# An attention + fp4 feed-forward block on one core: loads moved between two stacks of DMAs, and one small copy issued by ScalarE's own queue

## The reference

```
for each of the 16 batches b:
    q = layernorm(x[b])                       # no gain, no bias; eps 1e-5
    k = v = ctx[b]
    x1[b] = x[b] + softmax(q k^T / 4) v       # 16 heads of 16 channels
for each row of x1:
    z = layernorm(x1)
    h = silu(fp4(z) fp4(w_gate)^T) * (fp4(z) fp4(w_up)^T)    # 704 wide
    out = x1 + fp4(h) fp4(w_down)^T
# fp4: blocks of 16 along the last axis, scale = max|block| / 6, values on
# the grid 0, .5, 1, 1.5, 2, 3, 4, 6
```

## Time and profile before

| | |
|---|---|
| median of 3 runs | 541.68 us (538.37 to 542.48) |
| profiled execution, its own time | 540.0 us |
| its span | 538.2 us |
| attention: from the first scores of step 1 to those of step 13 | 53.82 to 230.52 us |
| mean granted TensorE clock | 0.975 |

### The profile page before, as it was taken

The page is one execution under the profiler, slowest core; times in us unless marked ns, Lnnn a source line. Parts: engine busy times, 40 slices in busy tenths (PEclk is TensorE's granted clock), DMA queues, the critical chain, the costliest instruction groups (busy, mean ns, idle before and its releaser), DMA issues.

```text
span 538.2 us, 13724 instructions
## 1 busy us (share of the span) xinstructions
PE 492.4 (91%) x4036; PEld 382.7 (71%) x4036; DVE 442.3 (82%) x1129; ACT 371.2 (69%) x739; POOL 306.0 (57%) x424
## 2 busy tenths in 40 slices
PE   1885999999999999999776799999999999999996
PEld 0232556556566666655445699999999999999996
DVE  3786799899998999988444789888899888899764
ACT  5355798989998999977663465666656665656653
POOL 7636566646556565533415565667666667666543
PEclk9999799999999999999876999999999999999999
DMA  7749658666667666530000000000000000000000
GB/s 213 221 131 234 185 141 226 191 174 185 185 184 186 187 196 196 154 102 22 3 0 2 0 12 21 19 19 19 10 19 19 19 19 19 10 19 21 22 22 29
DMA packets 49985, 48.97 MB, mean 91 GB/s; under 512 B 4768, under 2 KB 47648, under 8 KB 49952
## 3 DMA queue, kind: packets, MB, share of 16 engines
q1 hardware_dynamic: 49952, 48.58, 31.9%
HBM read 18.94 MB, written 4.19 MB: 43 GB/s over the span
## 4 chain that ended last, share of the span: by engine, by line
PE 72%; DVE 7%; SPq 5%; issue 5%; DMA 4%; POOL 3%; ACT 3%; DVEq 0%; POOLq 0%; ACTq 0%
PE SC L1172 21%; PE PV L1172 12%; PE PV L1120 9%; PE MX L1102 9%; PE SC L1088 8%; DVE MF L776 4%; PE T L1197 4%; SPq L299 3%; DMA QS<-MT 2%; PE T L1202 2%; PE T L1069 2%; PE T L1037 1%; PE SC L1197 1%; DMA KT<-in_ctx_t 1%; PE T L1044 1%
## 5 line engine op out<-in xcount | busy, mean ns | idle before, releaser
L776 DVE TENSOR_REDUCE MF<-MX 128x2 f32<-128x512 f32 x256 | 165.8, 683 | 20.9 <-PE MX L1102 17.3
L609 ACT ACTIVATE P<-SC 128x512 f32<-128x512 f32 x256 | 140.8, 593 | 26.8 <-PE SC L1088 25.2
L1102 PE MATMUL MX<-KS,QS 96*128 96x256 bf16 x512 | 104.3, 288 | 7.1 <-DVE MF L776 5.3
L1088 PE MATMUL SC<-QS,KS 98*128 98x256 bf16 x512 | 100.9, 280 | 5.9 <-DMA QS<-MT 5.8
L532 POOL TENSOR_TENSOR HQ<-HN,hscale 128x704 f32<-128x704 f32 x31 | 43.1, 1391 | 60.5 <-DVE HN L928 60.5
L1120 PE MATMUL PV<-P,VA 128*32 128x256 f32 x1024 | 72.0, 401 | 0.5 <-ACT OT L618 0.5
L1088 PEld LDWEIGHTS SC<-QS,KS 98*128 98x128 bf16 x512 | 44.2, 99 | 39.0 <-ACT P L609 17.3
L709 ACT ACTIVATE HH<-T 128x768 fp32r<-128x768 f32 x31 | 25.2, 813 | 67.1 <-PE T L1197 67.1
L1102 PEld LDWEIGHTS MX<-KS,QS 96*128 96x128 bf16 x512 | 43.3, 100 | 38.2 <-DVE MF L776 29.1
L1172 PE MATMUL SC<-WH,XH 128*128 128x352 f32 x256 | 68.3, 348 | 0.0
L1172 PE MATMUL SC<-WH,XL 128*128 128x352 f32 x256 | 62.6, 326 | 0.0
(11 more groups left out here) (137 smaller groups left out, 1034.4 us busy)
## 6 DMA issues: line engine op xcount, KB each, us to landing
KS<-KP SPq DMA_DIRECT2D x96, 128.0 KB, 2.9
QS<-QP SPq DMA_DIRECT2D x96, 128.0 KB, 2.4
QN<-in_x_p SPq DMA_DIRECT2D x16, 256.0 KB, 3.0
KT<-in_ctx_t SPq DMA_DIRECT2D x16, 256.0 KB, 3.1
C<-in_ctx SPq DMA_DIRECT2D x16, 256.0 KB, 4.2
X<-in_x SPq DMA_DIRECT2D x16, 256.0 KB, 4.6
out<-OB SPq DMA_DIRECT2D x32, 128.0 KB, 1.7
W<-in_L_ffn_w_down SPq DMA_DIRECT2D x2, 352.0 KB, 3.4
```

The source lines that it names most:

```text
L609: nc.scalar.activation(P[g % 2][:, j, :, :], SC[h % 3][:, :, :], ACT.Exp, scale=0.25).then_inc(exp_done, 1)
L776: nc.vector.tensor_reduce(MF[st.slot(off, 2)][:, :, h:h + 1], MX[h % 2][:, :, :], AX.X, ALU.max, negate=True).then_inc(mx_done, 1)
L1088: last = nc.tensor.matmul(SC[h % 3][:, k, :], KS[r][0:ROWS, h, k * 128:(k + 1) * 128], QS[r][0:ROWS, h, :], start=True, stop=True)
L1102: last = nc.tensor.matmul(MX[h % 2][:, q, :], QS[r][0:PROD, h, q * 128:(q + 1) * 128], KS[r][0:PROD, h, :], start=True, stop=True)
```

## The change

- **SyncE's order in a step** becomes: K stack, loads, Q stack, weights. The load of x is that of batch t and not t+1. The load of queries and keys of batch 3 (`load_first(3, 3)`) moves ahead of the first step. In step -1 the first weights come before the Q stack.
- **MT** is no longer in SyncE's order: ScalarE waits for its own copy to MT and issues the DMA itself, right behind it.
- **The rows of ones**: GpSimd writes KS[0] and KS[1] in step -2, one after the other, and KS[2] in step -1 once `v_ready` and `m_parts` (the maxima's low part of batch 0 on VectorE) are there. ScalarE writes KS[3] in step -1 at slot (1, 2), with one ACTIVATE over 2x4096 elements of a broadcast source, scale 0 and bias 1.
- **VectorE** waits for w_down's load at slot (3, 3) of step 4, and no longer at (1, 1).

```diff
--- before.py
+++ after.py
@@ -214,7 +214,7 @@
         w_zeroed, w_begun, w_loaded = sem("w_zeroed"), sem("w_begun"), [sem(f"w_loaded{m}") for m in range(3)]
         w_seq, w_scaled, w_abs, w_c, w_grid, w_done = (sem(n) for n in
             ("w_seq", "w_scaled", "w_abs", "w_c", "w_grid", "w_done"))
-        ones_ready = sem("ones_ready")
+        ones_ready, ones_last = sem("ones_ready"), sem("ones_last")
         w_tr, w_out = sem("w_tr"), sem("w_out")
         zeroed = sem("zeroed")
         wh_out = sem("wh_out")
@@ -350,16 +350,9 @@
             load_context(0, 0)
             sp.wait_ge(w_zeroed, 4)
             load_blocks(0, wg_in, 0, 2, w_begun)
+            load_first(3, 3)
 
             def attention_step(st):
-                if st.first >= 0 and st.has(RING):
-                    sp.wait_ge(v_ready, st.times(0, 1, 1))
-                    gate(sp)
-                    load_first(st.item(RING), st.slot(RING, RING))
-                if st.first >= 0 and st.has(2):
-                    load_context(st.item(2), st.slot(2, RING))
-                if st.first >= 0 and st.has(1):
-                    load_x(st.item(1), st.slot(1, RING))
                 if st.has(LEAD):
                     r = st.slot(LEAD, RING)
                     sp.wait_ge(k_low, st.times(LEAD, 1, 1))
@@ -367,22 +360,22 @@
                     sp.wait_ge(sc_ready, st.times(0, H, 1))
                     gate(sp)
                     stack(KS[r], KP[st.slot(LEAD, 2)], (0, 1, 2, 0, 1, 0), r)
-                if st.has(1):
-                    sp.wait_ge(mt_ready, st.times(1, 1, 1))
+                if st.first >= 0 and st.has(RING):
+                    sp.wait_ge(v_ready, st.times(0, 1, 1))
                     gate(sp)
-                    r = st.slot(1, 2)
-                    sp.dma_start(QS[st.slot(1, RING)][PROD:ROWS, :, :].rearrange("d h t -> d (h t)"),
-                                 MT[r][:, :]).then_inc(m_stacked[r], 16)
+                    load_first(st.item(RING), st.slot(RING, RING))
+                if st.has(2):
+                    load_context(st.item(2), st.slot(2, RING))
+                if st.has(0):
+                    load_x(st.item(0), st.slot(0, RING))
                 if st.first == -1:
-                    load_first(3, 3)
+                    load_weights(-1)
                 if st.has(LEAD):
                     sp.wait_ge(q_out, st.times(LEAD, 3, 3))
                     gate(sp)
                     stack(QS[r_q(st)], QP[st.slot(LEAD, 2)], (0, 0, 0, 1, 1, 2), r_q(st))
-                if st.first == -1:
-                    load_context(1, 1)
-                    load_x(0, 0)
-                load_weights(st.first)
+                if st.first >= 0:
+                    load_weights(st.first)
 
             def r_q(st):
                 return st.slot(LEAD, RING)
@@ -428,13 +421,11 @@
                 nc.gpsimd.memset(WD[:, r, FI:], 0.0).then_inc(w_zeroed, 1)
             pool.wait_ge(w_zeroed, 4)
 
-            def row_of_ones(r, st):
-
-                pool.wait_ge(k_low, st.first + LEAD + 1)
-                if st.has(1):
-                    pool.wait_ge(v_ready, st.first + 2)
-                nc.gpsimd.memset(KS[r][PROD:ROWS, :, :], 1.0).then_inc(ones_ready, 1)
-                pool.wait_ge(ones_ready, r + 1)
+            def rows_of_ones(rs):
+
+                for r in rs:
+                    nc.gpsimd.memset(KS[r][PROD:ROWS, :, :], 1.0).then_inc(ones_ready, 1)
+                    pool.wait_ge(ones_ready, r + 1)
 
             def attention_step(st):
                 if st.has(-2):
@@ -474,8 +465,13 @@
                     nc.gpsimd.tensor_scalar(VA[r][:, :, :, 0:DK],
                                             C[rc][:, :, :].rearrange("p q (h d) -> p q h d", d=DK),
                                             1.0, 0.0, ALU.mult, ALU.add).then_inc(v_ready, 1)
-                if 1 - LEAD <= st.first < 1 - LEAD + RING:
-                    row_of_ones(st.first + LEAD - 1, st)
+                if st.first == 1 - LEAD:
+                    pool.wait_ge(k_low, 2)
+                    rows_of_ones((0, 1))
+                if st.first == -1:
+                    pool.wait_ge(v_ready, 1)
+                    pool.wait_ge(m_parts, 1)
+                    rows_of_ones((2,))
                 if st.has(GRID):
 
                     ws = wslice(st, GRID)
@@ -598,6 +594,10 @@
                 if st.first + 1 >= 2:
                     act.wait_ge(m_stacked[r], st.turn(-1, 2, 16))
                 nc.scalar.activation(MT[r][:, :], TA16[0:2 * H, 0:S], ACT.Copy).then_inc(mt_ready, 1)
+                act.wait_ge(mt_ready, st.times(1, 1, 1))
+                gate(act)
+                nc.scalar.dma_start(QS[st.slot(1, RING)][PROD:ROWS, :, :].rearrange("d h t -> d (h t)"),
+                                    MT[r][:, :]).then_inc(m_stacked[r], 16)
 
             def exp(st, g, j):
                 if not st.has(0):
@@ -655,6 +655,11 @@
                         if (g, j) == (1, 2) and st.has(LEAD):
                             for q in range(QT):
                                 normalise(st, q)
+                        if (g, j) == (1, 2) and st.first == -1:
+                            act.wait_ge(consts, IDENTS)
+                            nc.scalar.activation(KS[RING - 1][PROD:ROWS, :, :].rearrange("d h t -> d (h t)"),
+                                                 ident[PROD:ROWS, 0:1].to_broadcast([ROWS - PROD, H * S]),
+                                                 ACT.Identity, bias=1.0, scale=0.0).then_inc(ones_last, 1)
                         if (g, j) == (2, 0) and st.first < 0:
                             maxima_out(st)
                         for n, at in enumerate(((2, 0), (2, 3), (3, 3))):
@@ -835,7 +840,6 @@
                     dve.wait_ge(w_loaded[0], 32)
                 elif st.first == RING:
                     dve.wait_ge(w_loaded[1], 48)
-                    dve.wait_ge(w_loaded[2], 32)
                 dve.wait_ge(w_scaled, st.times(SCALE, 1))
                 nc.vector.tensor_reduce(wmax[:, :], blocks(wslice(st, SCALE)), AX.X, ALU.max,
                                         apply_absolute_value=True).then_inc(w_seq, 1)
@@ -896,6 +900,8 @@
                             output(st, 1)
                         if (g, j) == ((3, 2) if st.first > 0 else (3, 3)) and st.has(SCALE):
                             weight_inverses(st)
+                        if (g, j) == (3, 3) and st.first == RING:
+                            dve.wait_ge(w_loaded[2], 32)
                         if st.first == B - 1 and HG * g + j < LOTS:
                             weights_out(HG * g + j)
 
@@ -1080,8 +1086,10 @@
                     if st.first == 0:
                         pe.wait_ge(ones_ready, 1)
                         pe.wait_ge(consts, CONSTS)
-                    if st.first in (1, 2, 3):
+                    if st.first in (1, 2):
                         pe.wait_ge(ones_ready, st.first + 1)
+                    if st.first == RING - 1:
+                        pe.wait_ge(ones_last, 1)
 
                 pe.wait_ge(exp_done, st.times(0, H, h - 2 if h > 2 else (0, -2, -1)[h]))
                 for k in range(QT):
```

## The result

| | median, us | range | runs | ratio to before, 95% interval |
|---|---|---|---|---|
| before | 538.67 | 535.1 to 542.48 | 20 | |
| changed | 543.13 | 541.39 to 545.65 | 20 | 1.0093 (1.007 to 1.0115) |

The change makes the kernel 0.9% slower. The median of before is that of 20 runs here; the 541.68 us given further up was of three. The profiled execution of the changed kernel took 542.69 us, with a span of 540.8 (before 540.0 and 538.2), so the two traces differ by 2.6 us, and this is what follows accounts for.

What follows compares the result with a forecast made beforehand. TensorE, busy 91% of the span, was taken as the bound, with ScalarE short of slack. 540.0 - 13.6 won + 7.0 paid = 533.4 us, or 534.5 for the middle of the runs; range 529 to 541.

Steps and rivals of the forecast that it cites:

- Loads behind the K stack: Each step, SyncE's order: four loads fit between K stack and Q stack, KT lands in time; cost put at nothing.
- (a): Before step 1: MT issued earlier by ScalarE lands before TensorE ends step 0; all 4.46 us of idle time go.
- MT on ScalarE's queue: Steps 0 to 14: issue and lost overlaps delay ScalarE 0.94 us, 0.55 us of pitch in steps 1 to 12; 7.0 us together.
- The first sum: Ahead of step 1: idle time before it, VectorE's slow cast and a TensorE stall in step 0 go; 6.8 us won.
- (b): Step -1: VectorE's cast of the maxima, no longer held by GpSimd's memset, takes 0.17 us instead of 1.47; 1.30 us won.
- (c): Step 0: the memset of ones is gone, and with it TensorE's stall at 47.36; 1.03 us won.
- The second sum: Steps 1 to 12: time above twelve pitches of 14.16 us (slow clock, w_down wait, late MT, memset) goes; 6.8 us won.
- Rival 2: Each step: ScalarE's issue waits for SyncE's, pitch grows by 1.18 us; 541 us, with half 537, written as 539; chance 0.20.
- Rival 3: Each step: the Q stack lands late behind the loads, pitch 16.0 at a 5.77 us landing; 548 us, slower; chance 0.10.
- Rival 4: Step 1: MT comes no sooner, the backlog being in the 16 engines; idle time and half clock stay; 540.5 us; chance 0.07.

## Why the prediction was wrong, point by point

**What bounds the kernel** was read rightly: TensorE, with ScalarE next in line and short of slack, and it is there that the kernel lost.

**The step that failed: "Loads behind the K stack ... Nothing, with the rival below."** I followed the landing of KT, of x and of the Q stack, and not that of MT, which the same loads are issued beside. In step (a) I had taken 2.8 us from the earlier trace rows as its flight, a row where MT has the K stack's tail ahead and no load after it, and set it down as good for the new order. It is 3.87 us. Of the pitch of 15.34, 14.88 is there with MT on ScalarE alone, so 0.46 us a step, 5.5 us in all, come from this. It was put at nothing, and it is the largest single miss: with it the profiled execution would have been forecast at about 539 us, and not at 533.4. The same "nothing" covered KT, and there too it is wrong at a pitch of 14.16 us, where ScalarE waited for KT for up to 3.27 us; the changed kernel's long step hides that.

**MT on ScalarE's queue: mechanism right, size off.** The exponentials and the copy of PV were pushed back, values at (3, 3) waited for the latter, and it was paid in each step. Forecast 0.94 us of delay for 0.55 of pitch, measured 0.72. The issue itself took 0.64 (0.69 taken); behind it ScalarE needs 0.2 us more before it starts, for which I had 0.1, so with the lost overlap the delay is 1.05 us. The pitch was mis-sized by 0.72 - 0.55 = 0.17 us, and 0.17 x 12 = 2 us.

**The first sum, 6.8 us ahead of step 1, came out as 4.35.** (a) The idle 4.46 us are gone, but through the order and not the queue (5.44 us under way with the old order). (b) The cast took 0.18 us:

```profile
27.29 0.18 DVE L802 CAST MP<-MF 128x32 bf16<-128x32 f32 x1
```

and the transposes of the maxima came 1.5 us earlier. That was lost at once: ScalarE's first issue, 1.49 us, held up the queries' part behind it, TensorE's next weights waited for that part, and the first scores came at 33.66, before at 33.55. The products at 31.33, with 1.28 us of idle time before them, name VectorE as their releaser; the weight load ahead of them names ScalarE's part:

```profile
30.92 0.10 PEld L1050 LDWEIGHTS T<-QP,negidentb 128*128 128x128 bf16 x1 [1.35 <-ACT QP L570]
```

(c) The stall in step 0 went, and two waits for ScalarE (0.51 and 0.45) took its place. So of the 2.44 us missing from this sum 1.41 are lost ahead of the first scores of step 0 and 1.03 between these and step 1.

**The second sum, 6.8 us above the pitch,** is gone as forecast in the changed kernel, since the longer pitch hides all small irregularities. Where the pitch is short, with MT on SyncE, 172.73 us for twelve steps leave 2.8 us, with the landings of the Q stack and of KT among them.

**The rivals.** Rival 2 gave the right pitch, 15.34 (14.16 + 1.18), and the right time within 2 us (541 with its full price), but by a mechanism that didn't occur: the issue took 0.64 us with SyncE's own beside it, so no wait for the other sequencer shows, and the shared generator of the Trainium skill, Perfetto Trace Analysis, section "DMA Instruction - HWDGE (DVE, Sync)", isn't needed to explain anything here. Rival 3 had the right cause, landings lengthened by the loads, and the wrong transfer. In the changed kernel the Q stack lands 2.5 us after its issue, and no wait of TensorE for it shows. It was late where the step is short: by 1.11 us in step 1 with MT on SyncE, and by 2.22 in step 3 of the kernel in which ScalarE only waits. Rival 4 is true of the queue (5.44 us under way in ScalarE's own) and false of the change, whose order took the backlog away. I had set 0.35 on no change and 0.10 on slower; a cost put at nothing and one above its middle lie on the same path, and the two together were not thought of.

**Not separated.** Whether MT ahead of the loads in SyncE's ring is quick because of its place in the ring or because SyncE starts the loads 1.0 us after it and not 0.07 was not tried. The changed kernel's own steps point to the head start: in steps 2 and 3, the two without a wait for MT, SyncE's first load was issued 1.47 and 0.66 us behind MT, and MT landed within 3.53 and 3.55 us (in step 0 these are 0.43 and 3.48); in the other steps from 1 to 12 the load was issued from 0.11 us ahead of MT to 0.23 behind it, and MT took 3.83 to 4.25.

## What to carry to other kernels

When a transfer is moved, list every transfer whose flight it will now overlap, and above all the small one that the next step starts with: a flight time read from a trace holds for the neighbours that it had there. An issue on a computing engine is a piece of work in that engine's order, here 0.95 us a time; on an engine with 0.2 us to give, all but that became the pitch here, and a queue of its own bought no shorter flight. And test the parts apart: all the edits but MT's took 0.9% off the time, and MT's alone put 1.8% on.

## What the runs showed that I had not expected

- The same 16 KB from ScalarE's queue: 2.31 us under way with nothing beside it, 3.87 with 1 MB of loads starting with it, 5.44 in the full engines of the prologue.
- ScalarE's first issue of the DMA of MT takes 1.25 to 1.49 us in all four kernels that have it as one DMA, later ones 0.63 to 0.67; to DRAM 0.36 the first time and then 0.31. With one DMA for each row the first is not slow: the second issue begins 0.64 us after it. Why is open.
- In the prologue TensorE's pairs of products took 0.63 us up to 38.9 us in the changed kernel and 0.39 from 33.3 us on in the one before, while the rows of the granted clock say 1.00 for both stretches; with MT on SyncE they took 0.63 up to 40 us. The idle times ahead of it differ (1.28 us at 31.33 in the changed kernel, 1.64 at 29.27 before). Why it changes pace where it does stays open; some 1.5 us of the prologue hang on it, an estimate from the times between the first scores of step 0 and those that follow the first values: 33.66 to 39.89 in the changed kernel, 33.55 to 39.12 with a stall of 0.88 us in it before.
- A memset of 2x4096 on GpSimd costs VectorE's cast from 0.8 to 3.4 us, according to where the two meet: the cast ends with the memset. Closing a seam elsewhere moved the cast of step 0 from just before the memset (42.46 and 43.04 us) onto its start.
- At a pitch of 14.16 us the keys' load, issued behind the K stack, is at the edge: ScalarE waited for it in every trace with the new order and that pitch, from 0.2 to 3.27 us at a time.
